# Two layers of a graph network on one core: control words of layer 1's sums packed three and six to a word, and the last stage's rows gathered into x's buffers

## The reference, cut to what matters

```python
gcn_out = jax.ops.segment_sum(norm[:, None] * h[src], dst, num_segments=n) + b_gcn
e = jax.nn.leaky_relu(al_src[src] + al_dst[dst], NEG_SLOPE)
ee = jnp.exp(e - emax[dst])
gat = jax.ops.segment_sum(att[..., None] * hg[src], dst, num_segments=n)
```

```python
_, idx = jax.lax.top_k(weights, k)
sel_idx = idx[:, :kk]
sel = jnp.take_along_axis(x, sel_idx[:, :, None], axis=1)
h = jax.nn.gelu(jnp.einsum('bkd,dh->bkh', sel, w1) + b1)
y = jnp.einsum('bkh,hd->bkd', h, w2) + b2
y = y * w_sel[..., None]
processed = jnp.zeros_like(x).at[batch_idx, sel_idx].set(y)
return processed + x
```

## Time and profile before

| | us |
|---|---|
| time, median of 3 runs | 8599.22 (8592.66 to 8604.39) |
| span of the profiled execution | 8601.4 |
| its own time | 8603.27 |
| PE busy in the span | 6543.5 (76%) |
| POOL busy | 3828.7 (45%) |
| DVE busy | 3556.7 (41%) |
| ACT busy | 1914.3 (22%) |

### The profile page before, as it was taken

The page is one execution under the profiler, slowest core; times in us unless marked ns, Lnnn a source line. Parts: engine busy times, 40 slices in busy tenths (PEclk is TensorE's granted clock), DMA queues, the critical chain, the costliest instruction groups (busy, mean ns, idle before and its releaser), DMA issues. The chain is left out here.

```text
span 8601.4 us, 109803 instructions
## 1 busy us (share of the span) xinstructions
PE 6543.5 (76%) x28541; PEld 4878.9 (57%) x28542; DVE 3556.7 (41%) x8183; ACT 1914.3 (22%) x4350; POOL 3828.7 (45%) x3997
## 2 busy tenths in 40 slices
PE   3797877887777899466688878771888776986677
PEld 2555555555547677443466656561666565766566
DVE  3211123333334222433355555547666555776200
ACT  1123420000001122111122222220123344661111
POOL 1567777777772000277677777761000000003111
PEclk9898878888875999578799998895999998995888
DMA  5776779999972000467677777762777665645110
GB/s 163 252 240 221 231 244 342 342 340 339 338 242 90 28 21 21 132 213 236 219 242 248 243 240 241 237 221 71 249 235 230 209 201 179 202 161 179 40 33 29
DMA packets 604940, 1708.05 MB, mean 199 GB/s; under 512 B 109370, under 2 KB 334479, under 8 KB 515140
## 3 DMA queue, kind: packets, MB, share of 16 engines
q1 hardware_dynamic: 338260, 981.33, 33.2%
q0 software_dynamic: 190752, 655.07, 24.0%
q10 hardware_dynamic: 75764, 69.93, 2.7%
HBM read 1084.38 MB, written 624.00 MB: 199 GB/s over the span
## 5 line engine op out<-in xcount | busy, mean ns | idle before, releaser
L723 POOL DMA_INDIRECT rows_ring<-h_rows,src_idx x1660 | 1730.5, 1042 | 651.0 <-issue 505.2
L1839 POOL DMA_INDIRECT x_sb<-xn_rows,src_tile x1563 | 1524.8, 976 | 473.4 <-issue 449.0
L816 PE MATMUL agg_ps_sum<-agg_rows,agg_sel_w 128*128 128x257 f32 x3080 | 1005.7, 475 | 266.0 <-DMA agg_rows<-edge_rows 183.7
L2610 PE MATMUL sums_ps_sum<-x_sb,sums_weighted 128*125 x4124 | 995.3, 397 | 264.2 <-DVE sums_weighted L2574 179.6
L2610 PEld LDWEIGHTS sums_ps_sum<-x_sb,sums_weighted 128*125 128x125 f32 x4124 | 780.5, 194 | 478.9 <-issue 355.3
L2574 DVE SCALAR_TENSOR_TENSOR sums_weighted<-x_sb 128x125 f32 x2062 | 720.5, 349 | 532.3 <-PE sums_ps_sum L2610 385.6
L816 PEld LDWEIGHTS agg_ps_sum<-agg_rows,agg_sel_w 128*128 128x128 f32 x3080 | 537.8, 219 | 509.4 <-issue 372.2
L792 DVE TENSOR_TENSOR agg_sel<-iota,dst_item 128x1280 bf16<-128x1280 f32 x166 | 250.6, 1509 | 881.0 <-PE agg_ps_sum L817 878.2
L2540 POOL DMA_INDIRECT node_tops<-tops,last_edge x98 | 93.4, 953 | 1118.4 <-DMA x_sb<-row_lots 1100.7
L2131 PE MATMUL mix_ps_h<-mix_x1t,mix_w 128*128 128x256 f32 x1600 | 386.7, 397 | 0.7 <-ACT mix_x1t L2193 0.7
L2642 ACT ACTIVATE sums_z<-sums_ps_sum 125x257 f32<-125x257 f32 x500 | 192.5, 385 | 857.8 <-PE sums_ps_sum L2610 771.5
(11 more groups left out here) (547 smaller groups left out, 11321.3 us busy)
## 6 DMA issues: line engine op xcount, KB each, us to landing
row_lots<-x_sb SPq DMA_DIRECT2D x195, 1048.0 KB
x_sb<-row_lots SPq DMA_DIRECT2D x195, 1048.0 KB
edge_rows<-rows_ring POOLq DMA_DIRECT2D x154, 1290.0 KB
agg_rows<-edge_rows SPq DMA_DIRECT2D x154, 1290.0 KB
sums<-sums_z ACTq DMA_DIRECT2D x500, 125.5 KB
fin_z<-sums SPq DMA_DIRECT2D x97, 642.5 KB, 3.8
xn_turned<-norm_xt SPq DMA_DIRECT2D x150, 256.0 KB, 2.1
rows_ring<-h_rows,src_idx POOLq DMA_INDIRECT x1660
```

What stands on the lines that cost most here:

```text
L723: pool.indirect_dma_start(self.ring[:, s, i, :], None, self.table, bass.IndirectOffsetOnAxis(g.src_idx[:, item:item + 1], 0)).then_inc(sel ...
L816: pe.matmul(ps[:, bass.ds(off, W)], sel_w[:, u, j, :], tiles[:, j, 0:W], start=False, stop=False, skip_group_check=True)
L1839: pool.indirect_dma_start(self.ring[:, s, i, :], None, g.xn_rows, bass.IndirectOffsetOnAxis(g.src_tile[:, tile:tile + 1], 0)).then_inc(sel ...
L2610: pe.matmul(ps[0:M, bass.ds(bank, SW)], weighted[:, s + j, :, :].rearrange("p n w -> p (n w)"), rows[:, bass.ds(off, SW)], start=False, st ...
```

## The change

It has three parts.

1. **Words.** An item's number, counted in the whole list, tells its set once its tile is known, because each item moves on by either one tile or one set. So DVE's word holds only tiles: the first tile in full and five distances of three bits, six items a word. PE's word holds three fields of eight bits (set modulo 8, and tile modulo 32), so that six items take two words; the top bits of the second hold the set number that the wait for ACT needs. In set_tables the item table has 18 columns in place of 17, laid out as 3 by 6, and the stores become 384 pairs of words for PE and 384 words for DVE in place of 2176 each. In sum_sets a part is 6 items, and both engines load for 72 items at once: 12 words for DVE, 24 for PE. The ring stays at 24.
2. **Node numbers.** POOL does one IOTA of 2500, and DVE writes the five stretches from it by adding 0, 2500, ... 10,000.
3. **Last stage.** All 50 tiles of picked rows get their own place in the buffer of x (`x_flat`, which is free by then), so a gather waits for nothing; POOL issues 16 ahead, and then four gathers before each scatter until all are issued. The MLP's weights are loaded during pick_rows, in buffers of an outer phase that spans both stages. The splitting of the bias stays where it was.

The diff, cut to its core:

```diff
+WORD_ITEMS = 6
+WORD_COLS = -(-SET_ITEMS // (WORD_ITEMS * P))
...
-                    act.dma_start(g.pe_words.rearrange("(k p) -> p k", p=P), words[:, :]).then_inc(words_moved, 16)
+                    act.dma_start(g.pe_words.rearrange("(k p h) -> p k h", p=P, h=2), words[:, :, :]).then_inc(words_moved, 16)
...
-                for k in range(SET_COLS):
+                for k in range(WORD_COLS * R):
                     done(dve.tensor_scalar(junk[:, 0:SETS - 1], starts[:, 1:SETS], item[:, k:k + 1], 0.0, ALU.is_le, ALU.add,
                                            accum_out=set_of[:, k:k + 1]))
...
-    PART = 8
-    PARTS = 3
-    STEP = PART * PARTS
+    PART = WORD_ITEMS
+    STEP = 24
+    LOAD = 3 * STEP
+    PARTS = LOAD // PART
...
-                for k in range(5):
-                    if k:
-                        pool.wait_ge(places, k)
-                    pool.iota(iota_i[:, :], pattern=[[1, 2500]], base=2500 * k, channel_multiplier=0).then_inc(iotas, 1)
-                    pool.wait_ge(iotas, k + 1)
-                    pool.tensor_copy(nodes[:, 2500 * k:2500 * (k + 1)], iota_i[:, :]).then_inc(places, 1)
+                pool.iota(iota_i[:, :], pattern=[[1, 2500]], base=0, channel_multiplier=0).then_inc(iotas, 1)
...
+                dve.wait_ge(iotas, 1)
+                for k in range(5):
+                    op = dve.tensor_scalar(nodes[:, 2500 * k:2500 * (k + 1)], iota_i[:, :], float(2500 * k), None, ALU.add)
+                op.then_inc(placed, 1)
...
-                def part(v, s, count):
-                    dve.wait_ge(rows_ready, ((v[count - 1] // (1 << 14)) & 255))
+                def tile_of(word, j):
+
+                    first = word % (1 << 11)
+                    return first if j == 0 else first + word // (1 << (8 + 3 * j)) % 8
+
+                def part(word, i, s, count):
+                    dve.wait_ge(rows_ready, ((tile_of(word, PART - 1) // LOT_TILES + 1) & 255))
                     for j in range(count):
-                        off = within(v[j] % (1 << 14), (EDGE_TILES - 1) * COLS)
-                        base = within((v[j] // (1 << 22)) * SET, NODES - SET)
+                        tile = tile_of(word, j)
+                        off = within(tile * COLS, (EDGE_TILES - 1) * COLS)
+                        base = within(tile * -SET + (i + j) * SET, NODES - SET)
...
                     pe.wait_ge(sel_ready, i + count)
-                    pe.wait_ge(free, (v[count - 1] // (1 << 15)) & 1023)
+                    pe.wait_ge(free, (words[1] // (1 << 21)) & 1023)
                     for j in range(count):
-                        off = within(v[j] % (1 << 15), (LOT_TILES * SUM_SLOTS - 1) * XROW)
-                        bank = within((v[j] // (1 << 15)) % BANKS * BANK, (BANKS - 1) * BANK)
+                        word, at = words[j // 3], 8 * (j % 3)
+                        low = word // (1 << at) if at else word
+                        off = within(low % 32 * XROW, (LOT_TILES * SUM_SLOTS - 1) * XROW)
+                        bank = within(word // (1 << (at + 5)) % BANKS * BANK, (BANKS - 1) * BANK)
...
+            @block.sync
+            def _(sp):
+                weights.load(sp, g)
+                sp.wait_ge(weights.loaded, 64)
+
...
-        rows = ph.sb("rows", [P, LOADS, 2 * C])
+        rows = g.x_flat.rearrange("p (t c) -> p t c", c=2 * C)
...
                 def gather(t):
-                    s = t % LOADS
-                    if t >= LOADS:
-                        pool.wait_ge(added, t // GROUP - LOADS // GROUP + 1)
-                    pool.indirect_dma_start(rows[:, s, :], None, g.pick_from, bass.IndirectOffsetOnAxis(g.pick_row[:, t:t + 1], 0)).then_inc(loaded[s], 16)
+                    pool.indirect_dma_start(rows[:, t, :], None, g.pick_from, bass.IndirectOffsetOnAxis(g.pick_row[:, t:t + 1], 0)).then_inc(loaded[t // GROUP], 16)
...
-                for t in range(PICK_GROUPS * GROUP):
+                AHEAD = 16
+                for t in range(AHEAD):
                     gather(t)
-                    if t >= LOADS and t % GROUP == 1:
-                        scatter(t - LOADS - 1)
-                        scatter(t - LOADS)
-                for t in range(PICK_GROUPS * GROUP - LOADS, PICK_TILES):
+                for t in range(PICK_TILES):
+                    for n in range(AHEAD + 4 * t, min(AHEAD + 4 * t + 4, PICK_GROUPS * GROUP)):
+                        gather(n)
                     scatter(t)
...
+                    pe.wait_ge(loaded[gi], 16 * GROUP)
                     for j in range(GROUP):
```

More of the change, by code:

```diff
@@ L1654, in _ @@
                 dve.tensor_scalar(lot_end[:, :], lot_sets[:, :], float(SET_ITEMS), None, ALU.min).then_inc(words_ready, 1)
[L1655 to L1659, removed]
@@ new lines, in _ @@
+                dve.wait_ge(step, n.up(4))
+                for h in range(2):
+                    done(dve.tensor_tensor(low[:, :, 3 * h], low[:, :, 3 * h], low[:, :, 3 * h + 1], ALU.bitwise_or))
+                for h in range(2):
+                    op = dve.tensor_tensor(words[:, :, h], low[:, :, 3 * h], field[:, :, 3 * h + 2], ALU.bitwise_or)
+                op.then_inc(words_ready, 1)
+                for j in range(1, R):
+                    op = dve.tensor_tensor(tile_f[:, :, j], tile_f[:, :, j], tile_f[:, :, 0], ALU.subtract)
@@ new lines, in _ @@
+                done(op)
+                done(dve.scalar_tensor_tensor(part_f[:, :], tile_f[:, :, 1], float(1 << 11), tile_f[:, :, 0], ALU.mult, ALU.add))
+                for j in range(2, R - 1):
+                    done(dve.scalar_tensor_tensor(part_f[:, :], tile_f[:, :, j], float(1 << (8 + 3 * j)), part_f[:, :], ALU.mult, ALU.add))
+                dve.tensor_copy(part[:, :], part_f[:, :]).then_inc(step, 1)
+                dve.tensor_copy(words2[:, :], tile_f[:, :, R - 1]).then_inc(step, 1)
@@ L1670, in _ @@
+                dve.wait_ge(step, n.up(2))
+                done(dve.tensor_scalar(words2[:, :], words2[:, :], 8 + 3 * (R - 1), None, ALU.logical_shift_left))
+                dve.tensor_tensor(words2[:, :], words2[:, :], part[:, :], ALU.bitwise_or).then_inc(words_ready, 1)
                 for m, (k0, k1) in enumerate(batches):
@@ L2991, in _, with __init__, load, last_mlp @@
                 dve.tensor_tensor(g.gain[:, :], w[:, :], g.picked[:, :], ALU.mult)
-def pick_rows(nc, g):
+class LastWeights:
+    def __init__(self, ph):
+        self.loaded = ph.sem("loaded")
+        self.w1 = ph.sb("w1", [P, KC, FF])
+        self.w2 = ph.sb("w2", [P, FF // P, C])
+        self.b1 = ph.sb("b1", [P, FF // P])
+        self.b2 = Bias(ph, "b2", C)
+    def load(self, sp, g):
+        load_all(sp, self.loaded, [
+            (self.w1[:, :, :], by_rows(g.given["L1_ffn_w1"])), (self.w2[:, :, :], by_rows(g.given["L1_ffn_w2"])),
+            (self.b1[:, :], columns(g.given["L1_ffn_b1"])), (self.b2.given[:, :], every(g.given["L1_ffn_b2"], BIAS_PARTS))])
+def last_mlp(nc, g):
+    with phase(nc, "mlp1") as ph:
+        weights = LastWeights(ph)
+        pick_rows(nc, g, weights)
+        ffn1(nc, g, weights)
+def pick_rows(nc, g, weights):
     T = TILES
```

135 lines of the change are left out of this document (69 added, 66 removed).

## The result

The changed kernel takes 8631.56 us (8623.58 to 8638.8, 5 runs) beside 8599.22 us before: a ratio of 1.0041, 95% interval 1.003 to 1.0053. It is slower by 0.4%, where 2% faster was forecast. The profiled execution has a span of 8637.0 us.

The account below looks back on a forecast made before the run. Sequencers of DVE and PE were taken to bound the sums' first stretch, ACT the second, row waits the last stage. Last stage -196.5, set_tables -12, sums +22 gave -186.5: 8414 us, range 8330 to 8495.

Parts of the forecast that it names:

- The last stage: Pick and last stage: PE's groups back to back, 15.07 us each; 186 saved, 11 more by an earlier start; -196.5 in all.
- Rival 3: Last stage: PE loses its clock or waits a little each group, 17 us a group; +48, time 8462, chance .09.
- set_tables: Table-building stage: fewer small stores save 15 us, added DVE work costs 3; net -12, ends -7 and -18.
- The stores: In set_tables: 1024 elements written in place of 4608; 15 us saved, between 10 and 21.
- The DVE operations: In set_tables: one pass more and some 14 more small operations; together +3 us.
- The start of the sums: Node numbers converted by DVE from one IOTA, five conversions of 1.65 us; 12 us by the sum, -10 taken.
- DVE's item: Sums loop: .50 us a middle item, .57 an item on average with load and branch, so DVE sets the pace.
- the forecast of the sums: First to last product: +20 us in the first stretch and +12 in the second.
- The second half: Second stretch of the sums: 798 items at .57 take 455 us, under ACT's 535; +12, between 0 and 30.
- rival 4: Sums: DVE's sequencer at .70 us an item or more gives +208, slower overall; at .72 time 8631; chance .04.
- The words of PE: Sums loop: PE needs .48 us an item, its two register instructions staying below the product's pitch, under DVE's .57.

Follow-up runs that it names:

- experiment 5: Changed kernel with turns of 48 items and DVE's address arithmetic written four ways, for items 1 to 4 of a part; sums 1339.7 us.
- experiment 8: Changed kernel with turns of 48 items and a subtraction in place of the negative product in the set's offset; sums 1350.1 us, ratio to before 0.9884.
- experiment 9: Changed kernel, turns of 72 items kept, with a subtraction in place of the negative product alone; sums 1336.5 us against 1495.5.
- experiment 2: Changed kernel with turns of 24 items in place of 72 on both engines; sums 1383.1 us against 1495.5.
- experiment 3: Changed kernel with turns of 48 items in place of 72; sums 1349.3 us against 1495.5.
- experiment 7: Kernel of experiment 4 with DVE's loop body written out three times, 72 items a turn; sums 1212.5 us.
- experiment 6: Kernel of experiment 4 with DVE's loop body written out four times, 96 items a turn; sums 1274.9 us.
- experiment 1: Kernel before with the last stage's part of the change alone; 8399.26 us beside 8595.18, ratio 0.9774.
- experiment 4: Changed kernel with DVE back to one word an item, turns of 24; PE's new words in turns of 72; 8356.24 us beside 8595.18, ratio 0.9725.

## Why the prediction was wrong

By its own steps:

**The last stage: right.** A group was to take 15.07 us at full clock; the timeline has 15.02 from one turn to the next, and 32 first products in 7.07:

```profile
8345.15 0.66 PE L3201 MATMUL ffn_ps_t<-ident,x_sb 128*128 128x128 f32 x4
8345.64 7.07 PE L3226 MATMUL ffn_ps_h<-ffn_xt,mlp_w 128*128 128x256 f32 x32
...
8360.17 0.66 PE L3201 MATMUL ffn_ps_t<-ident,x_sb 128*128 128x128 f32 x4
```

PE's time from start to last product is 380 as forecast, and the first turn stands 67.0 us behind the pick's IOTA, 78.0 before: 11. Rival 3, by which the clock would still fall at small idle times, did not come about: from 8300 to 8600 PE has none, and the granted clock was 1.00. So the rule of the Trainium skill, "TensorE: Matmul & The Clock Gate", section "A second HAM failure mode: psum-queue depth-cycling", wasn't put to the test: it speaks of small idle times between groups.

**set_tables: right in sum.** The stores:

```profile
3523.90 0.38 ACTq L1586 DMA_DIRECT2D pe_words<-sets_words  x1
...
3535.71 0.21 DVE L1499 COPY ranges_cnt<-deg_cnt 128x98 f32<-128x98 f32 x1 [9.25 <-PEq L115]
```

```profile
3527.50:3535.50 8.00, 0.00 (x0) 0.00 (x0) 0.00 (x0) 0.00 (x0) 0.00 (x0) 0.50 0.00 0
```

11.8 us from the first store's issue to the next operation, 26.6 before: 14.8 saved, where I had taken 15, between 10 and 21. The second fence is a window: by the packets' own times the last of them ends at 3527.4, and 8.3 us without traffic follow; before, the last ended at 3531.1, and 12.3 followed (not the 13 that I had read). So traffic gave 11 us and the silent rest 4: it shrinks too where there are fewer small writes. The rule of the Trainium skill, "DMA: Bandwidth & Descriptors", section "Anatomy of one DMA — SWDGE (gpsimd) path", had led to the lower saving, 10; the measurement decides for more. The DVE operations cost 2 us in place of 3.

**The start of the sums: mis-sized by 5.**

```profile
5964.04 6.94 DVE L2579 TENSOR_SCALAR x_sb<-sums_iota_i 128x2500 uint16<-128x2500 int32 x5 [1.86 <-POOL sums_iota_i L2551]
5972.84 0.35 DVE L2601 SCALAR_TENSOR_TENSOR sums_weighted<-x_sb 128x125 f32<-128x125 uint16 x1 [1.86 <-issue]
```

Five conversions take 6.94 us, 1.39 each, against 1.65 from the earlier trace rows and 2.27 on POOL. My own sum had given 12; I took 10 for a slower conversion that didn't come.

**DVE's item: the step that failed, for .57 read .725.** It has two mistakes.

The first is the step "The first holds a division, a remainder and four simple operations, as the one of .180 does: .19". That price was too low even for the instructions that I had read, those of the first turn, which stands outside the loop and has the counter as a constant. One middle item of it in the trace:

```profile
L2601 DVEq FUSED_REGOPS  x2: 99/188/276, 5974.0 to 5974.3; - x2
...
L2601 DVEq ALU_OP  x1: 40/40/40, 5974.4 to 5974.4; - x1
```

.276 for the .19, and .55 us from matrix to matrix for the .50. Inside the loop the item's number is a register, and (i + j) * 25 is computed anew for each item: 7, 6 and 3 operations in place of 6, 6 and 1. The three instructions then take .307, .093 and .065, and the distance is .60. The part's first item with the head takes some .91 (.78 forecast), the last .45 (.38), so a part takes 3.76 where the sum had 3.25. So of a middle item's .10, half was wrong already in the first turn, and half came with the counter. Why the instruction of .276 is so much dearer than the one of .180, with as many operations by the code, stays open (experiments 5 and 8). The price of a loop without any gap is what experiment 9 shows: 1336.5 us, .648 an item. That is 105 us over the 1231 of before and some 73 over the forecast of the sums (+32).

The second is a cost that the sum doesn't have at all: the code of a turn. I had counted operations, loads and branches, and wrote that the loads stand "every 72 items" as a gain, with .6 us for a branch. The branch costs 6 us when DVE's turn has 318 instructions, and nothing at 295 or less. 1495.5 - 1336.5 = 159 us in 27 turns behind a branch, 5.9 each. Experiments 2, 3, 7 and 9 (110, 214, 248 and 295 instructions, no gap) and experiment 6 (330, a gap, with the old arithmetic) separate it from the decode. Whether the length alone decides, or also where in the program the loop stands, is taken up at the end.

73 + 159 = 232, the whole of the miss.

**The second half.** I had costed it at ACT's pace with +12. With DVE at .725 an item ACT's pace doesn't bind, and the slow sequencer is paid for all 2062 items. That is rival 4, with the chance of .04: "It decides from .70 on; at .72 the time is 8631". Its place, DVE's item at .70 us or more, was right. That its time is the measured 8631.56 is luck: it had laid the whole to register instructions, and 159 us of the 264.5 came from the code's length, which no rival had.

**The words of PE: right and small.** PE's fused instructions took .14 us in the median, .096 before, and PE's loop showed no gap, but PE was never the limit.

## What to carry to other kernels

Cost a loop's body as it stands in the loop, not in its first, unrolled turn: the counter is a register there, and terms that were constants become instructions on every item. When a body is written out more times to save loads or branches, count its instructions on each engine and look behind the branch in the sequencer's records; here 318 instructions in place of 295 cost 159 us. And a decode that moves work from memory to registers pays only on an engine whose sequencer has time: DVE's had .37 us an item for .35 of work and could carry nothing more, PE's could, so the mixed version (one word an item for DVE, three a word for PE) won.

## What the runs showed of the hardware that was not expected

- DVE's sequencer runs a loop of 295 instructions with .21 us behind its branch, and one of 318 with 6.0 us; each such turn adds 5 packets of 8 KB to the instruction queue ((235 - 103) / 27). PE ran a loop of 472 instructions with .06 us behind its branch. Why the engines differ wasn't tried.
- The limit isn't one number. A loop of exactly 300 instructions in the stage behind the sums, the same code in all kernels, had 2.93 us behind its branch in the kernel before (the same in experiments 1 and 3), 2.96 in experiment 8, and some .25 in the changed kernel and in all others. Its place in the program moved, and I know of nothing else that did. In the kernel before its four turns take 64.7 us in place of 62.5, some 9 us in all, more than the -5.7 that the table leaves over. With the sums' own loop short, the instruction queue then has some 20 packets more, again 5 a turn (123 in experiment 8, 103 in experiments 7 and 9).
- The places fit one reading, which no run was made to test. Where DVE meets code for the first time, the hold-ups of .4 us stand exactly 128 instructions apart (in the changed kernel's loop at the 41st, 169th and 297th behind the branch), and the queue's packets have 8 KB. Counted in pieces of 128 from the hold-ups, the loop of 318 starts 87 into a piece and touches four, and so does that of 330 in experiment 6; the loop of 295, from the same start, ends 2 instructions before the fourth; those of 84 to 248 touch three or fewer. The loop of 300 starts 88 to 110 into a piece in the kernels where it has the gap (four pieces), and 16 to 63 where it hasn't (three); in experiment 5 and in both traces of experiment 4's kernel it has none and starts within one instruction of a boundary, which my count can't resolve. So in the other traces a loop has the gap just where it touches a fourth piece. By this reading 318 instructions would have cost nothing in another place; why such a turn moves five packets it doesn't say.
- DVE's fused register instructions, in ns: with three simple operations 65 to 71, with five 88, with six 93 to 99; with a division and a remainder among six 180 in the kernel before and 267 to 282 in the changed one's first turn, among seven 300 to 307 in its loop. A division alone took 68, a mask alone 45. The differences don't make a list of prices (experiments 5 and 8).
